# Each query-major score tile of self-attention made twice into its bank, in a decoder layer on one core

## The chip, the cores and the metric

The kernel runs on one core of one Trainium2 chip. The metric is the device time of one execution in microseconds; lower is better. "Before" is the kernel as it stands, "after" the kernel with the change below.

## What is computed

One decoder layer in fp32 for 4 sequences of 256 tokens and 128 channels: self-attention with l2-normed queries and keys, cross-attention with relative positions, and a top-1 mixture of 8 experts, each with a residual and a layer norm. The change lies in the self-attention:

```python
q = l2norm(q); k = l2norm(k)                         # over all 128 channels
q, k, v = (t.reshape(b, n, H, D).transpose(0, 2, 1, 3) for t in (q, k, v))   # H = 16 heads, D = 8
attn = jnp.einsum('bhnd,bhkd->bhnk', q * scale, k * scale) / temperature
attn = jax.nn.softmax(attn, axis=-1)
out = jnp.einsum('bhnk,bhkd->bhnd', attn, v)
```

## The kernel before

The five engines run programs of their own and meet at semaphores. What each does, and when, follows one table, ORDER, of steps "stage.step.batch": A1 and A2 are the self-attention of a batch, B its cross-attention and router, W work for later (blank stores, weight loads). Each engine goes through ORDER and takes the steps that concern it, in that order, so the work of up to three batches is interleaved on TensorE. After the table come the expert tiles (`up`, `down`).

The softmax needs each query's maximum over the keys. For that the scores are made query-major: step A1.d0 to A1.d15 of a batch, one tile per pair of heads and half of the queries. In `scores1` TensorE makes a tile with two matmuls (bf16 parts of the fp32 operands, 96 rows of contraction, 128 queries, 256 keys), one for each head, into the two halves of one bank of SA. VectorE reduces the bank to two negated maxima per query (`maxima`, L980). SA has two banks, and the tiles take them in turn together with the key-major tiles (A2.st0 to st15, `scores_t`, L1251, read by ScalarE's exponential at L761): `score_bank` makes TensorE wait until the tile two turns earlier has been read. The maxima are transposed (A1.shT, L1183), written to DRAM and read back as an extra row of the queries' operand, so that the key-major tiles come with the maximum already subtracted. Tiles of the exponential are multiplied with the values in `weigh1` (A2.pv, L1262).

Names that the rows show: SA the two score banks; negm the maxima; KS, QS the stacked operands of even batches and w_sb those of odd ones (they lie in the weights' room); MA and MB boxes of PSUM that one use after another fills; SB the four banks of cross-attention; L1345 and L1349 its scores, L1368 the subtraction of its maxima, L1051 its reduction, L1046 the maximum of two of its tiles, L801 and L798 its exponentials, L1380 its product with the values; L1215 the matmuls that stack the heads of batch 0, copied out by ScalarE (L708, L741); L1195 the projection of x; L603 the blank stores from P2b to sorted_x, issued by GpSimd when TensorE's count of score tiles has come to a point in ORDER; L425 SyncE's loads.

Of the kernel before, what the change touches and what calls it, by code (L numbers as in the profile page):

```python
# [13 lines left out]
NB, NT, C = 4, 256, 128  # L14
H, D = 16, 8
P = 128
# [6 lines left out]
SR = NTERM * D  # L23
# [32 lines left out]
def steps_of(text):  # L56
# [35 lines left out]
    B.tr5.3 W.v5.0 B.sc6.3 B.sh5.3 B.tr6.3 B.sc7.3 B.pv0.3 B.sh6.3 B.tr7.3 B.rk.2 B.sh7.3 B.nm0.3 B.pv1.3  # L92
    B.nm1.3 B.ln2.3 B.x2T.3 B.lg.3 B.rk.3
""")


A_FILLS = {"A1.qkv": ("qkv0", "qkv1"), "A1.qkT": ("qkT",), "A2.pv1": ("pv0",), "A2.nm0": ("norm0",), "A2.k2T": ("k2T",),
# [53 lines left out]
def column_a(g, j):  # L151

    return 8 * (j // 4) + 4 * g + j % 4
# [10 lines left out]
def build(nc, x_rows, x_cols, ctx_cols, wqkv_t, temperature, wproj_t, proj_b, wq_t, bq, wk_t, bk, wv_t, bv,  # L164
          er_t, router_w, router_b, w1, b1_cols, w2, b2, out):
    ctx = ExitStack()
    with ctx:
# [3 lines left out]
        def sb(name, shape, dt=FP32):  # L171
            return ctx.enter_context(nc.sbuf_tensor(name, shape, dt))

        def pb(name, shape, dt=FP32):
            return ctx.enter_context(nc.psum_tensor(name, shape, dt))

        def sem(name):
            return ctx.enter_context(nc.semaphore(name))
# [59 lines left out]
        QSs, KSs = (QS0, QS1), (KS0, KS1)  # L238
# [58 lines left out]
        start = sb("start", [P, E])  # L297
# [37 lines left out]
        def as_fp32(tile):  # L335
# [25 lines left out]
        SA = pb("SA", [P, 2, 512])  # L361
# [7 lines left out]
        s = {n: sem(n) for n in (  # L369

            "wqkv_in", "w_in", "temp_in", "c_in", "er_in", "fill", "stack0_fill", "pick_ok", "odd_ok", "ex_full", "ex_out", "v1_fill", "ident_ok", "consts", "er_split", "er_stacked", "bigw",
            "dchain", "pchain",

            "ma_full", "ma_free", "mb_full", "mb_free",

            "xT_in", "xtok_in", "n2_ok", "n2c_ok", "rn_ok", "qkn_ok", "v1_ok", "xpb_ok", "spa_ok", "pa_out", "qs_in",
            "stack_fill", "sa_full", "negm1_ok", "m_out0", "m_out1", "m_in0", "m_in1", "st_full", "exp1", "ve1_ok", "rs1_ok", "x1_ok",
# [801 lines left out]
        def _(pe):  # L1179
            mm = nc.tensor.matmul  # L1180
# [38 lines left out]
            def score_bank(name, b, u):  # L1219

                turn = TURN[name, b, u]
                if turn >= 2:
                    last_name, last_b, last_u = SCORES[turn - 2]
                    wait(pe, {"d": "negm1_ok", "st": "exp1"}[last_name], last_b * 16 + last_u + 1)
                return turn % 2

            def scores1(b, u):

                hp, qt = divmod(u, 2)
                if b == 0 and qt == 0:  # L1230
                    pe.wait_ge(s["ex_out"], hp + 1)
                if b > 0 and u == 0:
                    pe.wait_ge(s["qs_in"], b * 64)
                bank = score_bank("d", b, u)
                for i in range(2):
                    last = mm(SA[:, bank, i * NT:(i + 1) * NT], QSs[b % 2][0:2 * SR, column_a(i, hp), qt * P:(qt + 1) * P], KSs[b % 2][0:2 * SR, hp, :],  # L1236
                              start=True, stop=True)
                last.then_inc(s["sa_full"], 1)

            def transpose_shifts(b, a):  # L1240
# [4 lines left out]
            def scores_t(b, u):  # L1245

                hp, kt = divmod(u, 2)
                if u % 8 == 0:
                    pe.wait_ge(s[f"m_in{u // 8}"], b * 16 + 16)
                bank = score_bank("st", b, u)  # L1250
                mm(SA[:, bank, :], KSs[b % 2][:, hp, kt * P:(kt + 1) * P], QSs[b % 2][:, column_a(0, hp):column_a(1, hp) + 1:4, :], start=True, stop=True).then_inc(s["st_full"], 1)  # L1251

            def weigh1(b, grp):
                if grp == 0:
# [193 lines left out]
            def rank_then(b):  # L1448
                rank(b)
                keep_busy(b, "rk")  # L1450

            turns({
                ("A1", "qkv"): project_x, ("A1", "qkT"): transpose_q_k, ("A1", "ex"): stack_heads, ("A1", "d"): scores1, ("A1", "shT"): transpose_shifts,
                ("A1", "vcp"): first_weights, ("A2", "q2T"): project_q2,
                ("A2", "st"): scores_t, ("A2", "pv"): weigh1, ("A2", "nm"): transpose_o, ("A2", "oT"): o_to_cols,
                ("A2", "proj"): project_o, ("A2", "x1T"): x1_to_cols, ("A2", "k2T"): project_k2,
                ("B", "v"): project_v2, ("B", "gt"): stack_queries, ("B", "sc"): scores2, ("B", "tr"): transpose_scores, ("B", "sh"): shift,
# [92 lines left out]
```

## Time and profile before

| | |
|---|---|
| median of 3 runs | 312.88 us (311.1 to 313.0) |
| profiled execution | 311.56 us, span 309.8 us, 1.76 us around it |
| TensorE matmul busy | 247.2 us (80%), 3439 instructions |
| VectorE busy | 213.1 us (69%), 592 instructions |
| ScalarE busy | 137.1 us (44%) |
| mean granted TensorE clock | 0.888 |

A row of the timeline has the start in the span, the duration, the engine, line and operation, what is written from what, the shape, and how many instructions were merged into it; in brackets stands how long the engine was idle before it and what ended that. Matmuls overlap: of several in a row each shows its full latency, while their starts lie closer together.

### The profile page before, as it was taken

The page shows a single profiled execution, that of the slowest core. Times are in us where ns is not written, and L with a number is a line of the kernel's source. Part 1 is how long each engine was busy: PE and PEld are TensorE (multiplying, and loading weights), DVE is VectorE, ACT ScalarE, POOL GpSimd, SP SyncE. Part 2 cuts the span into 40 slices and gives each one's busy share as a digit, 9 for nine tenths or more (in the row PEclk, how much of TensorE's full clock was granted, in tenths as well). Part 3 has the DMA queues.
Part 4 walks back from the last instruction along what each step waited for, and adds up shares of the span by engine and source line. Part 5 has one row for each costly group of instructions (what it writes and reads, how often), then busy time and mean ns, then how long its engine had stood idle before and what let it go on. Part 6 is the DMA issues. An engine that isn't in the chain of part 4 may idle for free.

```text
span 309.8 us, 8568 instructions
## 1 busy us (share of the span) xinstructions
PE 247.2 (80%) x3439; PEld 185.4 (60%) x3440; DVE 213.1 (69%) x592; ACT 137.1 (44%) x318; POOL 81.0 (26%) x120
## 2 busy tenths in 40 slices
PE   3068797768999689997978999779786599999950
PEld 1037423322778466774867777569675359999950
DVE  8868955885677586797687745565343385899980
ACT  3127556306554445763332777523344213454420
POOL 8310400172011012074000030203103020456562
PEclk9999959955899989998779999995969958999995
DMA  2301488935688530269551013732710103499200
GB/s 68 118 0 51 160 288 215 254 91 95 168 226 220 146 51 20 87 190 234 90 133 26 4 49 92 138 104 45 263 38 9 29 17 87 132 307 359 83 6 1
DMA packets 28726, 36.36 MB, mean 117 GB/s; under 512 B 6039, under 2 KB 22405, under 8 KB 28016
## 3 DMA queue, kind: packets, MB, share of 16 engines
q1 hardware_dynamic: 24624, 23.67, 30.3%
q0 software_dynamic: 4064, 12.16, 11.7%
q8 instruction: 27, 0.44, 0.6%
q14 instruction: 11, 0.09, 0.1%
HBM read 24.41 MB, written 11.80 MB: 117 GB/s over the span
## 4 chain that ended last, share of the span: by engine, by line
PE 42%; DVE 9%; issue 5%; ACT 3%; DMA 3%; POOL 1%; SPq 1%; POOLq 0%; DVEq 0%; ACTq 0%
PE SB L1349 5%; PE SA L1488 5%; PE SB L1345 4%; PE SB L1488 4%; PE MB L1183 4%; PE SB L1496 3%; PE MB L1380 3%; PE SA L1323 2%; PE SB L1368 2%; DVE negm L980 2%; PE MA L1262 2%; DMA w_sb<-parts_a 2%; PE SA L1251 2%; PE SA L1236 2%; DMA parts_a<-SpA 1%
## 5 line engine op out<-in xcount | busy, mean ns | idle before, releaser
L980 DVE TENSOR_REDUCE negm<-SA 128x2 bf16<-128x512 f32 x64 | 41.4, 686 | 10.4 <-PE SA L1236 9.9
L761 ACT ACTIVATE P<-SA 128x512 f32<-128x512 f32 x64 | 35.8, 598 | 12.6 <-PE SA L1251 11.3
L708 ACT ACTIVATE Sb<-SB 128x512 bf16<-128x512 f32 x24 | 14.3, 597 | 36.0 <-PE SB L1349 35.9
L1051 DVE TENSOR_REDUCE negm<-MB 128x4 bf16<-128x512 bf16 x32 | 22.0, 687 | 9.2 <-PE MB L1183 8.9
L801 ACT ACTIVATE P2b<-SB 128x1024 f32<-128x1024 f32 x16 | 16.4, 1024 | 12.5 <-PE SB L1368 8.5
L654 POOL TENSOR_TENSOR rs<-ve,half 128x2 f32<-128x2 f32 x8 | 5.7, 712 | 57.2 <-DVE ve L941 57.2
L1046 DVE TENSOR_TENSOR Sm<-SB,Sb 128x512 bf16<-128x512 f32 x16 | 11.0, 688 | 13.9 <-ACT Sb L708 13.7
L1262 PE MATMUL MA<-P,V 128*32 128x256 f32 x256 | 19.0, 433 | 0.4 <-ACT qkT L708 0.4
L1368 PE MATMUL SB<-identb,negm 128*128 128x128 bf16 x192 | 18.0, 240 | 1.5 <-DVE negm L1051 1.5
L1236 PE MATMUL SA<-w_sb 96*128 96x256 bf16 x64 | 14.5, 332 | 5.7 <-DVE negm L980 3.6
L1195 PE MATMUL MA<-wqkv,xT 128*128 128x384 f32 x16 | 10.1, 726 | 10.0 <-ACT qkv L708 4.9
L695 POOL DMA_INDIRECT out<-P,token x15 | 15.4, 1030 | 6.0 <-issue 6.0
L1368 PEld LDWEIGHTS SB<-identb,negm 128*128 128x128 bf16 x192 | 13.9, 108 | 4.5 <-DVE negm L1051 2.9
L708 ACT ACTIVATE P<-MA 128x128 f32<-128x128 f32 x15 | 4.2, 278 | 28.0 <-PE MA L1183 19.0
L1349 PE MATMUL SB<-QZ,ErS 128*128 128x32 bf16 x384 | 15.8, 194 | 0.7 <-issue 0.7
L1349 PE MATMUL SB<-Z,ErS 128*128 128x32 bf16 x384 | 15.6, 194 | 0.0
L677 POOL DMA_INDIRECT sorted_x<-x,slot x8 | 8.2, 1024 | 27.9 <-DVE slot L1090 26.7
L1345 PE MATMUL SB<-QZ,KS 128*128 128x32 bf16 x384 | 13.8, 181 | 1.3 <-DVE QZ L1031 1.3
L690 POOL TENSOR_TENSOR rs<-ve,half 128x1 f32<-128x1 f32 x15 | 8.9, 595 | 20.6 <-DVE ve L1163 20.6
L1183 PE MATMUL MB<-identb,Sm 128*128 128x128 bf16 x96 | 10.0, 230 | 5.4 <-DVE Sm L1046 4.0
L1345 PEld LDWEIGHTS SB<-QZ,KS 128*128 128x128 bf16 x384 | 12.5, 100 | 2.4 <-issue 1.3
L1349 PEld LDWEIGHTS SB<-QZ,ErS 128*128 128x128 bf16 x384 | 13.4, 104 | 0.8 <-issue 0.8
(247 smaller groups left out, 607.9 us busy)
## 6 DMA issues: line engine op xcount, KB each, us to landing
sorted_x<-P2b POOLq DMA_DIRECT2D x4, 1161.0 KB, 6.7
w_sb<-in_w POOLq DMA_DIRECT2D x8, 512.0 KB, 4.7
w_sb<-in_w POOLq DMA_DIRECT2D x8, 256.0 KB, 4.3
w_sb<-parts_a SPq DMA_DIRECT2D x8, 192.0 KB, 4.0
parts_b<-SpB SPq DMA_DIRECT2D x8, 192.0 KB, 2.4
KZ<-parts_b SPq DMA_DIRECT2D x4, 384.0 KB, 5.3
Z<-parts_b SPq DMA_DIRECT2D x4, 384.0 KB, 5.5
KS<-parts_b SPq DMA_DIRECT2D x4, 384.0 KB, 5.5
```

What stands on the lines that cost most here:

```text
L708: return a.activation(dst, src, ACT.Copy)
L761: a.activation(P1[:, grp % 2, kt, 2 * i:2 * i + 2, :].rearrange("p h t -> p (h t)"), SA[:, bank_a("st", b, u), :], ACT.Exp).then_inc(s["ex ...
L801: a.activation(P2b[:, :, :, qs].rearrange("p k h q -> p (k h) q"), SB[:, at:at + 2, :].rearrange("p k (h q) -> p (k h) q", h=H), ACT.Exp). ...
L980: v.tensor_reduce(out=negm1[:, hp // 4, qt, :, hp % 4], in_=SA[:, bank_a("d", b, u), :].rearrange("p (g k) -> p g k", g=2), axis=AX.X, op= ...
L1051: v.tensor_reduce(out=negm2[:, qb, :], in_=MBb[:, 0:512].rearrange("p (c k) -> p c k", c=4), axis=AX.X, op=ALU.max, negate=True).then_inc( ...
L1183: return nc.tensor.transpose(dst, src, idn)
L1236: last = mm(SA[:, bank, i * NT:(i + 1) * NT], QSs[b % 2][0:2 * SR, column_a(i, hp), qt * P:(qt + 1) * P], KSs[b % 2][0:2 * SR, hp, :], sta ...
L1262: last = mm(MA[VW * i:VW * i + VW, (grp % 2) * NT:(grp % 2 + 1) * NT], V1[:, kt, h, :], P1[:, grp % 2, kt, i, :], start=(kt == 0), stop=(k ...
L1345: mm(bank[:, h, :], keys[:, h, kt * P:(kt + 1) * P], queries[:, h, QB * qb:QB * (qb + 1)], start=(h == 0), stop=False, skip_group_check=True)
L1349: last = mm(bank[:, :, q:q + 2], ErS[:, w:w + P], queries[:, :, QB * qb + q:QB * qb + q + 2], start=False, stop=False, skip_group_check=True)
L1368: last = mm(SB[:, banks_b(qb)[kt], c * P:(c + 1) * P], negm2[:, qb, c:c + 1].broadcast_to([P, P]), identb[:, :], start=False, stop=True, s ...
L1488: last = mm(UP[par][bank][:, k * P:(k + 1) * P], weights[:, at:at + P], xgT[:, par, :], start=True, stop=True)
```

## The change

Each of the 64 query-major tiles (16 in each of 4 batches) is made twice in a row by the same two matmuls into the same bank. Both rounds have start=True, so the second overwrites the first; the semaphore that releases VectorE is raised by the last matmul of the second round. The key-major function has the same loop, but no key-major step is in the table, so it runs once. Nothing is moved: each engine keeps its order. The lines of the changed file lie 15 or more further down.

```diff
+TWICE = frozenset("""
+    A1.d0.0 A1.d1.0 A1.d2.0 A1.d3.0 A1.d4.0 A1.d5.0 A1.d6.0 A1.d7.0 A1.d8.0 A1.d9.0 A1.d10.0 A1.d11.0 A1.d12.0
...
+def times(stage, step, b):
+
+    return 2 if f"{stage}.{step}.{b}" in TWICE else 1
...
                 bank = score_bank("d", b, u)
-                for i in range(2):
-                    last = mm(SA[:, bank, i * NT:(i + 1) * NT], QSs[b % 2][0:2 * SR, column_a(i, hp), qt * P:(qt + 1) * P], KSs[b % 2][0:2 * SR, hp, :],
-                              start=True, stop=True)
+                for _ in range(times("A1", f"d{u}", b)):
+                    for i in range(2):
+                        last = mm(SA[:, bank, i * NT:(i + 1) * NT], QSs[b % 2][0:2 * SR, column_a(i, hp), qt * P:(qt + 1) * P], KSs[b % 2][0:2 * SR, hp, :],
+                                  start=True, stop=True)
                 last.then_inc(s["sa_full"], 1)
```

## Rows read from the trace of the kernel before

**Rows 1.** The page: busy time, and the chain by engine.

```profile
PE 247.2 (80%) x3439; PEld 185.4 (60%) x3440; DVE 213.1 (69%) x592; ACT 137.1 (44%) x318; POOL 81.0 (26%) x120
...
PE 42%; DVE 9%; issue 5%; ACT 3%; DMA 3%; POOL 1%; SPq 1%; POOLq 0%; DVEq 0%; ACTq 0%
```

**Rows 2.** Line L1236: durations in ns (min/median/max), and what ended its waits.

```profile
L1236 PE MATMUL SA<-KS,QS x64: 269/273/418, 25.4 to 118.8; 96*128 96x256 bf16 x64
...
  DVE negm L980: 15.9, 30
```

**Rows 3.** Timeline, batch 0's tiles: VectorE.

```profile
33.14 3.81 DVE L980 TENSOR_REDUCE negm<-SA 128x2 bf16<-128x512 f32 x6 [0.37 <-PE SA L1236]
```

**Rows 4.** Timeline, batch 0's tiles: TensorE.

```profile
30.38 0.82 PE L1215 MATMUL SB<-SpA,P2b 128*96 128x256 bf16 x6
...
35.24 0.90 PE L1236 MATMUL SA<-KS,QS 96*128 96x256 bf16 x4 [0.37 <-DVE negm L980]
37.01 0.22 PE L1183 MATMUL MA<-identb,negm 128*16 128x128 bf16 x1 [0.86 <-DVE negm L980]
```

**Rows 5.** Timeline, batch 1's tiles: TensorE.

```profile
53.76 0.39 PE L1236 MATMUL SA<-w_sb 96*128 96x256 bf16 x2 [0.65 <-DVE negm L980]
...
67.14 1.20 PE L1236 MATMUL SA<-w_sb 96*128 96x256 bf16 x4 [1.90 <-DVE negm L980]
68.54 1.21 PE L1236 MATMUL SA<-w_sb 96*128 96x256 bf16 x4 [0.19 <-DVE negm L980]
```

**Rows 6.** Timeline, batch 1's tiles 8 to 15: VectorE.

```profile
66.40 5.47 DVE L980 TENSOR_REDUCE negm<-SA 128x2 bf16<-128x512 f32 x8
```

**Rows 7.** A window at batch 2's tiles 0 to 3: us, PE, PEld, DVE, ACT, POOL, clock, DMA.

```profile
90.20:94.50 4.30, 4.28 (x94) 3.78 (x91) 3.19 (x7) 1.89 (x4) 0.72 (x1) 1.00 0.45 116
```

**Rows 8.** Timeline, batch 2's tiles 3 to 9: TensorE, ScalarE, GpSimd.

```profile
94.10 0.38 PE L1236 MATMUL SA<-KS,QS 96*128 96x256 bf16 x2
...
94.78 0.75 POOL L603 DMA_DIRECT2D sorted_x<-P2b  x1 [2.89 <-PE SA L1236]
...
103.83 1.02 ACT L801 ACTIVATE P2b<-SB 128x1024 f32<-128x1024 f32 x1 [3.85 <-DMA sorted_x<-P2b]
...
105.78 0.91 PE L1195 MATMUL MA<-wqkv,xT 128*128 128x384 f32 x2 [3.02 <-ACT qkv L708]
...
109.16 1.06 PE L1236 MATMUL SA<-KS,QS 96*128 96x256 bf16 x4
```

**Rows 9.** Timeline, TensorE behind batch 2's tiles 11 and 12.

```profile
115.05 0.62 PE L1368 MATMUL SB<-identb,negm 128*128 128x128 bf16 x8 [0.20 <-DVE negm L1051]
```

**Rows 10.** Timeline, batch 3's tiles: TensorE.

```profile
144.83 1.03 PE L1236 MATMUL SA<-w_sb 96*128 96x256 bf16 x4 [1.70 <-DMA w_sb<-parts_a]
...
158.66 0.61 PE L1183 MATMUL MB<-identb,Sm 128*128 128x128 bf16 x4 [1.40 <-DVE Sm L1046]
...
162.85 0.39 PE L1236 MATMUL SA<-w_sb 96*128 96x256 bf16 x2 [0.31 <-DVE negm L980]
```

**Rows 11.** Windows at half clock: us, busy of PE, PEld, DVE, ACT, POOL, clock, DMA.

```profile
62.80:79.80 17.00, 13.35 (x55) 4.88 (x59) 12.25 (x27) 5.53 (x11) 8.02 (x15) 0.50 0.43 90
...
107.10:110.50 3.40, 3.40 (x65) 2.98 (x62) 1.49 (x4) 2.44 (x7) 1.02 (x1) 0.50 1.07 207
...
158.30:161.70 3.40, 3.04 (x25) 2.78 (x26) 2.88 (x5) 1.02 (x1) 0.00 (x0) 0.50 0.65 133
```

**Rows 12.** Timeline, TensorE: a key-major tile and a step weigh1 at either clock.

```profile
42.42 3.52 PE L1262 MATMUL MA<-P,V 128*32 128x256 f32 x32
...
75.28 0.61 PE L1251 MATMUL SA<-w_sb 128*128 128x512 bf16 x1 [0.16 <-ACT P L761]
...
86.47 0.39 PE L1251 MATMUL SA<-w_sb 128*128 128x512 bf16 x1 [0.16 <-ACT P L761]
...
77.58 3.01 PE L1262 MATMUL MA<-P,V 128*32 128x256 f32 x32 [0.41 <-ACT qkT L708]
...
88.13 1.93 PE L1262 MATMUL MA<-P,V 128*32 128x256 f32 x32
```

More of the change, by code:

```diff
@@ L94 @@
 """)
+TWICE = frozenset("""
+    A1.d0.0 A1.d1.0 A1.d2.0 A1.d3.0 A1.d4.0 A1.d5.0 A1.d6.0 A1.d7.0 A1.d8.0 A1.d9.0 A1.d10.0 A1.d11.0 A1.d12.0
+    A1.d13.0 A1.d14.0 A1.d15.0 A1.d0.1 A1.d1.1 A1.d2.1 A1.d3.1 A1.d4.1 A1.d5.1 A1.d6.1 A1.d7.1 A1.d8.1 A1.d9.1
+    A1.d10.1 A1.d11.1 A1.d12.1 A1.d13.1 A1.d14.1 A1.d15.1 A1.d0.2 A1.d1.2 A1.d2.2 A1.d3.2 A1.d4.2 A1.d5.2
+    A1.d6.2 A1.d7.2 A1.d8.2 A1.d9.2 A1.d10.2 A1.d11.2 A1.d12.2 A1.d13.2 A1.d14.2 A1.d15.2 A1.d0.3 A1.d1.3
+    A1.d2.3 A1.d3.3 A1.d4.3 A1.d5.3 A1.d6.3 A1.d7.3 A1.d8.3 A1.d9.3 A1.d10.3 A1.d11.3 A1.d12.3 A1.d13.3 A1.d14.3
+    A1.d15.3
+""".split())
+def times(stage, step, b):
+    return 2 if f"{stage}.{step}.{b}" in TWICE else 1
 A_FILLS = {"A1.qkv": ("qkv0", "qkv1"), "A1.qkT": ("qkT",), "A2.pv1": ("pv0",), "A2.nm0": ("norm0",), "A2.k2T": ("k2T",),
@@ L1250, in scores_t @@
                 bank = score_bank("st", b, u)
-                mm(SA[:, bank, :], KSs[b % 2][:, hp, kt * P:(kt + 1) * P], QSs[b % 2][:, column_a(0, hp):column_a(1, hp) + 1:4, :], start=True, stop=True).then_inc(s["st_full"], 1)
+                for _ in range(times("A2", f"st{u}", b)):
+                    last = mm(SA[:, bank, :], KSs[b % 2][:, hp, kt * P:(kt + 1) * P], QSs[b % 2][:, column_a(0, hp):column_a(1, hp) + 1:4, :], start=True, stop=True)
+                last.then_inc(s["st_full"], 1)
             def weigh1(b, grp):
```

## The prediction

> **What bounds the kernel now.** I read the page first, then the line of the doubled matmul, then the timeline around each batch's tiles, engine by engine. TensorE is busy for 80% of the span and holds 42% of the chain that ended last [rows 1]; VectorE reduces each tile. So the question for each of the 64 tiles is which of three things runs there: TensorE without a pause (then the added matmuls are paid in full), the loop over the two banks (then a part of them), or an engine or a transfer that TensorE waits for anyway (then nothing).
>
> **What one tile more costs.** A matmul of this line lasts 269 ns and more, at most 418 [rows 2], but matmuls overlap, and it is the distance of their starts that counts. A pair at full clock takes 0.38 us to its end [rows 8]; less 0.27 that is 0.11 from start to start. Four at half clock take 1.06 us [rows 8], so (1.06 - 0.42)/3 = 0.21. The change adds 2 matmuls to each tile: 0.21 us at full clock, 0.43 at half clock, and as much to the time until VectorE may begin. 64 times 0.21 is 13.7 us, which is the added issue time if the clock were full all along. The weight loads are the same weights again and run beside the matmuls. Nothing else is added, no wait and no transfer.
>
> **Batch 0 (25.4 to 37.0 us): bank loop.** VectorE makes 6 reductions in 3.81 us [rows 3]: (3.81 - 0.69)/5 = 0.62 a tile, 1.25 for a pair of tiles. That looks like VectorE's bound, but TensorE's rows show that it is just as much the loop of one bank: a reduction of 0.69, some 0.06 to 0.15 until TensorE starts, 0.38 for the tile, 0.04 until VectorE reads, together 1.2 to 1.26. VectorE therefore has no reserve of its own that would hide the second round; the loop grows by 0.21 to about 1.47. Where six matmuls of L1215 stand between two pairs of tiles (0.82 us to the end of the last, so 0.11 from start to start [rows 4]), TensorE alone needs 8 + 6 matmuls of 0.107 = 1.50 for what now takes 1.25. Seven such steps by 0.22, and 0.1 for the first pair: **+1.6 us**. TensorE waits 0.86 us for the last reductions before it can go on [rows 4], so the stretch is on the path. Bounds: 7 times 0.05 (were the six matmuls and the pauses to take it all) = 0.4, and 16 times 0.21 = 3.4.
>
> **Batch 1, tiles 0 to 7 (52.5 to 58.8).** TensorE waits for the banks again, 0.65 us before tile 2 [rows 5], and other steps of the same batch (the transposes of the outputs, the projection) stand between the tiles. Tile 0 comes 0.21 later, the loop of its bank adds 0.15 to 0.21 once more before each of two VectorE steps that the projection needs; the rest lies in the waits: **+0.6**, bounds 0.2 and 8 times 0.21 = 1.7.
>
> **Batch 1, tiles 8 to 15 (64.2 to 72), at half clock.** The first two are made long before VectorE is free: TensorE then waits 1.90 us [rows 5], so their second round is hidden. The other six are three rounds of the bank loop. It shows best here: TensorE starts at 67.14 and 68.54 [rows 5], 1.40 apart, which is 0.69 + 0.06 + 0.60 + 0.04, and VectorE's 8 reductions take 5.47 [rows 6]. At half clock the loop grows by 0.43 to 1.82. 3 times 0.43 and a remainder for the last tile: **+1.5** if the clock stays as it is. Bounds 0 and 8 times 0.43 = 3.4.
>
> **Batch 2, tiles 0 to 7 (90 to 101.5).** Up to 94.5 TensorE is busy 4.28 of 4.30 us [rows 7], so tiles 0 to 3 cost their full 4 times 0.21 = **+0.85**. Then comes a transfer: the last blank store is issued at 94.78, once tile 3 is made, ScalarE waits for it 3.85 us until 103.83, and TensorE behind it 3.02 us until 105.78 [rows 8]. Whatever tiles 4 to 7 add between 98.6 and 101.5, 0.85 us in all, disappears in those 3.02 us: **0**. Without that cover it would be 0.85.
>
> **Batch 2, tiles 8 to 15 (109 to 119).** Tiles 8 and 9 stand in an unbroken row of matmuls at half clock [rows 8]: 2 times 0.43 = **+0.85** (0.43 at full clock). Behind tiles 10 to 14 TensorE waits for VectorE's other reduction (0.20 us before 115.05 [rows 9], with the bank waits of tiles 12 to 14 before and behind it), and tile 15 lies beside a copy of ScalarE: **0**, at most 6 times 0.21 = 1.3.
>
> **Batch 3 (144.8 to 168).** Tile 0 begins when its operands land, after a wait of 1.70 us, and again at half clock: four matmuls take 1.03 [rows 10]. Tiles 0 to 2 add 1.28, of which some 0.2 lie in the wait for a bank: +1.1. Tile 3 is on the path, tile 4 keeps VectorE supplied and counts no further: +0.2. Tiles 5 to 7 end in TensorE's wait of 1.40 us for VectorE before 158.66 [rows 10]: 0. Tiles 8 and 9 are at half clock among matmuls of cross-attention: +0.85. Tiles 10 to 12 push the bank wait of 0.31 [rows 10] along: +0.3. Tiles 13 to 15: +0.45. Together **+2.9**, bounds 1.5 and 16 times 0.21 plus 5 times 0.21 for the tiles at half clock = 4.4. After 168 us there are no such tiles and everything moves as one.
>
> **The sum at the old clocks** is 1.6 + 0.6 + 1.5 + 0.85 + 0.85 + 2.9 = +8.3 us.
>
> **The clock.** From 62.8 to 79.8 us TensorE has half clock and is busy 13.35 of 17.0 us; the stretch 107.1 to 110.5, with 3.40 of 3.40, ends at once, and so does 158.3 to 161.7 with 3.04 of 3.40 [rows 11]. All three follow a stretch in which TensorE waited. With the second round, tiles 10 to 15 leave TensorE next to no pause (8 matmuls of 0.213 = 1.71 in a loop of 1.82), which the rows of the two short stretches liken to those that ended. So I take it that full clock comes back around tile 14 and not at 79.8. That returns 0.4 at tiles 14 and 15; 3.01 - 1.93 = 1.1 in the step that multiplies with the values [rows 12]; and some 0.5 in the key-major tiles, whose matmul is 0.61 - 0.39 = 0.22 shorter [rows 12], in two to three rounds of their loop. **-2.0.** The forecast is 8.3 - 2.0 = +6.3: 311.56 + 6.3 = **317.9 us** for an execution like the profiled one, which is 1.3 us below the median of the runs shown; 317.9 is 1.6% above that median. I give it without an addition for that, since one of those runs lies at 311.1.
>
> The Trainium skill says in "TensorE: Matmul & The Clock Gate", part 1, that "the default state is throttled, and activity releases the throttle". By that rule an added matmul can pay for itself. The trace agrees as far as its half-clock stretches follow waits; it cannot show how much more activity would have sufficed.
>
> **The rivals.**
> (a) The clock does not come back earlier: +8.3 at the old clocks, 319.9 us. For it: in the 17 us at half clock TensorE was already busy for 79% of the time [rows 11] and the clock stayed down.
> (b) Not slower: the clock. Besides the stretch above, TensorE's added work keeps the clock up at 107.1 to 110.5 and 158.3 to 161.7, where it is busy all the time [rows 11] and so would need about half: 1.7 + 1.5 us, of which 2 times 0.85 less 0.43 each, 0.85, was counted above as half-clock cost of the tiles and goes too; and 1.5 at batch 0's multiplication with the values, which took 3.52 us [rows 12]. 6.3 - 3.2 - 0.85 - 1.5 = +0.7, 312.3 us. It decides from where the added rounds fill the waits ahead of those stretches; the waits of 3.02 and 1.40 us [rows 8, 10] are longer than the 0.85 and 0.64 added in front of them, which speaks against it. In part it gives 314 to 316.
> (c) VectorE hides nearly all of it: the tiles wait for VectorE, not it for them. Then only the 4 + 2 + 4 tiles with TensorE unbroken count: about +2.5, 314 us. Against it: the loop of 1.40 us in batch 1 leaves VectorE idle between pairs of reductions.
> (d) All on the path: waits that I took for cover are loops that stretch along. 13.7 plus 0.21 for each of some 15 tiles at half clock: +17, 328 us. Against it: the 3.02 us behind the blank store.
> (e) The second round isn't made, or runs beside something: the program order of the changed kernel shows it as instructions of its own, 256 instead of 128. 312 us.
>
> **How the numbers follow.** Forecast 0.53 (315.9 to 319.5), (a) 0.18, (b) 0.14, (c) 0.08, (d) 0.06, (e) 0.01. The range from 313.0 to 322.5 holds the forecast, (a) with the bounds of the single stretches, (c) and the milder half of (b), and leaves out (d) and the rest. About 1%, 3.1 us, is what a measurement of this kernel can tell from no change. Slower by over 1% means above 316.0: most of the forecast, (a) and (d): 0.75. Within 1%: (b), (c), (e) and the lower edge of the forecast: 0.22. Faster: 0.03, if (b) goes further than worked out.
>
> **What the profile after would show.** TensorE's line with 256 matmuls, its starts 0.11 apart; batch 0's reductions no longer end to end but in pairs 1.47 apart; the blank store issued 3 to 4 us later than 94.78, with TensorE's wait behind it shorter by about 0.85; no longer wait behind tiles 5 to 7 of batch 3; and the half-clock stretch of batch 1 shorter than 17 us. Wrong would be: VectorE's last 6 reductions of batch 0 in the same 3.8 us, or a clock that falls and rises elsewhere by more than the sum.

## The result, and the profile after

| | before | after |
|---|---|---|
| median | 312.9 us, 4 runs (311.1 to 313.0) | 319.72 us, 4 runs (318.52 to 321.75) |
| profiled execution, span | 311.56 us, 309.8 us | 321.75 us, 320.0 us |
| mean granted TensorE clock | 0.888 | 0.913 |

The ratio is 1.027, with an interval of 1.020 to 1.034: slower. A repeat on one of the chips of the experiments, below, gave 1.012 (1.003 to 1.022). The medians differ by 6.8 us; the forecast was 6.3 us over the profiled execution, 317.9 us, and 319.72 lies inside the range of 313.0 to 322.5. Ratios below are made from undisturbed executions alone, so they are not always the quotient of the medians given with them. The unchanged kernel spreads more than those four runs show: on the three chips of the experiments its executions took 307.8 to 323.5 us.

The page after, its busy times and its chain by engine (before: [rows 1]):

```profile
PE 256.5 (80%) x3567; PEld 197.8 (62%) x3568; DVE 213.9 (67%) x592; ACT 136.8 (43%) x318; POOL 81.1 (25%) x120
...
PE 55%; DVE 16%; DMA 10%; issue 7%; ACT 5%; SPq 3%; POOL 1%; another core or an unknown queue 1%; POOLq 0%; ACTq 0%; DVEq 0%
```

TensorE has 128 matmuls more and 9.3 us more of busy time, and 12.4 us more of weight loads, which run beside the matmuls; the other engines are within 0.8 us of before. The line of the doubled matmul, durations in ns and then its waits and who waited for it:

```profile
L1252 PE MATMUL SA<-KS,QS x128: 269/272/289, 25.4 to 126.8; 96*128 96x256 bf16 x128
...
  DVE negm L995: 8.1, 18
...
  DVE negm L995: 18.0, 22
```

The first of the two waits is TensorE's for VectorE's reductions, the second VectorE's for TensorE. The first has halved, from 15.9 us in 30 places [rows 2] to 8.1 in 18, and the second has grown from 9.9 us to 18.0. The 15.9 and 8.1 count the weight load and the matmul behind it both; of the matmuls alone the wait fell from 4.8 to 2.1 us. A part of the second round lies in that difference. The rest is paid. Batch 0, VectorE and then TensorE (before: [rows 3, 4]):

```profile
34.68 1.29 DVE L995 TENSOR_REDUCE negm<-SA 128x2 bf16<-128x512 f32 x2 [0.55 <-PE SA L1252]
36.21 1.29 DVE L995 TENSOR_REDUCE negm<-SA 128x2 bf16<-128x512 f32 x2 [0.24 <-PE SA L1252]
37.68 1.29 DVE L995 TENSOR_REDUCE negm<-SA 128x2 bf16<-128x512 f32 x2 [0.18 <-PE SA L1252]
```

```profile
34.04 1.04 PE L1252 MATMUL SA<-KS,QS 96*128 96x256 bf16 x8
34.91 0.82 PE L1230 MATMUL SB<-SpA,P2b 128*96 128x256 bf16 x6
35.57 1.07 PE L1252 MATMUL SA<-KS,QS 96*128 96x256 bf16 x8
37.05 1.12 PE L1252 MATMUL SA<-KS,QS 96*128 96x256 bf16 x8 [0.41 <-DVE negm L995]
39.03 0.27 PE L1198 MATMUL MA<-identb,negm 128*16 128x128 bf16 x1 [0.86 <-DVE negm L995]
41.85 1.03 PE L1268 MATMUL SA<-QS,KS 128*128 128x512 bf16 x2 [2.55 <-DMA QS<-shift_a]
```

Six reductions that ran end to end in 3.81 us now come in pairs 1.53 and 1.47 us apart, with VectorE waiting for TensorE in between. On TensorE 8 + 6 matmuls fill 34.04 to 35.57, the 1.53 of the pairs, and the wait of 0.86 us ahead of the transposition is the same as before: the stretch moved as one. The last row is a wait that the forecast did not have, 2.55 us for the read of the maxima; it is followed up below.

Batch 1, VectorE and TensorE at half clock (before: [rows 5, 6]):

```profile
72.94 0.69 DVE L995 TENSOR_REDUCE negm<-SA 128x2 bf16<-128x512 f32 x1 [0.54 <-PE SA L1252]
...
74.76 0.69 DVE L995 TENSOR_REDUCE negm<-SA 128x2 bf16<-128x512 f32 x1 [0.27 <-PE SA L1252]
...
76.58 0.69 DVE L995 TENSOR_REDUCE negm<-SA 128x2 bf16<-128x512 f32 x1 [0.27 <-PE SA L1252]
```

```profile
68.84 1.91 PE L1252 MATMUL SA<-w_sb 96*128 96x256 bf16 x8
71.86 5.54 PE L1252 MATMUL SA<-w_sb 96*128 96x256 bf16 x24 [1.11 <-DVE negm L995]
...
83.83 1.93 PE L1280 MATMUL MA<-P,V 128*32 128x256 f32 x32 [0.41 <-ACT qkT L723]
...
98.62 0.61 PE L1252 MATMUL SA<-KS,QS 96*128 96x256 bf16 x4 [3.06 <-DMA KS<-parts_a]
```

Every second reduction stands 1.82 us behind the one before, against 1.40 of the bank's loop before, and 24 matmuls make a row without a pause. The wait behind tiles 8 and 9 fell from 1.90 to 1.11 us: their second round was hidden. At 83.83 full clock was back, and the step that multiplies with the values took 1.93 us, against 3.01 before [rows 12]; in the four other profiles with this batch doubled the step stood wholly in half clock and took 3.64. The last row is another wait that before did not have, ahead of tile 0 of batch 2.

Batches 2 and 3, GpSimd, ScalarE and TensorE (before: [rows 8, 10]):

```profile
103.98 0.75 POOL L618 DMA_DIRECT2D sorted_x<-P2b  x1 [4.28 <-PE SA L1252]
```

```profile
110.61 1.02 ACT L816 ACTIVATE P2b<-SB 128x1024 f32<-128x1024 f32 x1 [0.51 <-PE SB L1386]
```

```profile
113.91 0.91 PE L1210 MATMUL MA<-wqkv,xT 128*128 128x384 f32 x2 [0.66 <-ACT qkv L723]
...
152.89 1.05 PE L1252 MATMUL SA<-w_sb 96*128 96x256 bf16 x8 [1.04 <-DMA w_sb<-parts_a]
...
165.52 0.61 PE L1198 MATMUL MB<-identb,Sm 128*128 128x128 bf16 x4 [1.18 <-DVE Sm L1061]
165.92 1.06 PE L1252 MATMUL SA<-w_sb 96*128 96x256 bf16 x4
```

The blank store was issued 9.2 us later than before, at 103.98, and had landed when ScalarE needed it at 110.61: ScalarE waited for TensorE instead (0.51, against 3.85 for the store before), and TensorE's wait behind it fell from 3.02 to 0.66. The wait for VectorE ahead of tiles 8 and 9 of batch 3 fell only from 1.40 to 1.18, less than the 0.64 that the prediction put into it. The windows at half clock and one of the stretches that were at half clock before (us, busy of PE, PEld, DVE, ACT, POOL, clock, DMA; before: [rows 11]):

```profile
66.40:83.40 17.00, 14.64 (x49) 6.53 (x49) 11.01 (x25) 5.08 (x11) 8.06 (x15) 0.50 0.42 90
165.40:168.80 3.40, 3.28 (x24) 2.79 (x25) 2.12 (x5) 0.92 (x1) 0.00 (x0) 0.50 0.86 159
112.00:120.00 8.00, 7.25 (x158) 5.90 (x157) 6.14 (x14) 3.88 (x12) 1.02 (x1) 1.00 0.54 124
```

TensorE was busy for 14.64 of 17.00 us instead of 13.35, and half clock still lasted 17.00 us. The page and these rows already decide three of the signs named beforehand: VectorE's pairs 1.47 us apart came, a half-clock stretch shorter than 17 us did not, and the blank store was later by 9.2 instead of 3 to 4 us, 3.1 of it from the wait ahead of batch 2.

### The profile page after: what moved, and what is told of

Its sections match the earlier page's. It is cut to its first block, busy times and chain, and to the rows that moved or that the text cites. A ratio compares the mean times of both kernels' runs of the same rounds, so it can differ in the third digit from the quotient of the medians.

```text
span 320.0 us, 8824 instructions
## 1 busy us (share of the span) xinstructions
PE 256.5 (80%) x3567; PEld 197.8 (62%) x3568; DVE 213.9 (67%) x592; ACT 136.8 (43%) x318; POOL 81.1 (25%) x120
## 3 DMA queue, kind: packets, MB, share of 16 engines
q0 software_dynamic: 4064, 12.16, 11.2%
## 4 chain that ended last, share of the span: by engine, by line
PE 55%; DVE 16%; DMA 10%; issue 7%; ACT 5%; SPq 3%; POOL 1%; another core or an unknown queue 1%; POOLq 0%; ACTq 0%; DVEq 0%
PE SA L1252 7%; PE SB L1367 6%; PE SA L1506 5%; PE SB L1363 5%; PE MB L1198 4%; PE SB L1506 4%; PE MB L1398 4%; DMA w_sb<-parts_a 4%; PE SB L1514 3%; DVE negm L995 3%; PE SA L1268 3%; SPq L440 3%; PE MA L1198 2%; DMA KS<-parts_a 2%; PE MA L1210 2%
## 5 line engine op out<-in xcount | busy, mean ns | idle before, releaser
L995 DVE TENSOR_REDUCE negm<-SA 128x2 bf16<-128x512 f32 x64 | 42.4, 688 | 18.5 <-PE SA L1252 18.0
L723 ACT ACTIVATE Sb<-SB 128x512 bf16<-128x512 f32 x24 | 14.3, 597 | 41.1 <-PE SB L1367 38.5
L1252 PE MATMUL SA<-w_sb 96*128 96x256 bf16 x128 | 22.2, 319 | 3.9 <-DMA w_sb<-parts_a 2.0
L1061 DVE TENSOR_TENSOR Sm<-SB,Sb 128x512 bf16<-128x512 f32 x16 | 11.0, 688 | 16.6 <-ACT Sb L723 15.5
L1252 PE MATMUL SA<-KS,QS 96*128 96x256 bf16 x128 | 17.7, 273 | 3.9 <-DMA KS<-parts_a 3.1
L1252 PEld LDWEIGHTS SA<-w_sb 96*128 96x128 bf16 x128 | 12.6, 111 | 11.1 <-DVE negm L995 5.3
L1386 PE MATMUL SB<-identb,negm 128*128 128x128 bf16 x192 | 16.7, 228 | 1.3 <-DVE negm L1066 1.3
L710 POOL DMA_INDIRECT out<-P,token x15 | 15.5, 1031 | 6.0 <-issue 6.0
L1280 PE MATMUL MA<-P,V 128*32 128x256 f32 x256 | 16.3, 383 | 0.4 <-ACT qkT L723 0.4
L1252 PEld LDWEIGHTS SA<-KS,QS 96*128 96x128 bf16 x128 | 11.2, 97 | 7.6 <-DMA KS<-parts_a 3.2
L1386 PEld LDWEIGHTS SB<-identb,negm 128*128 128x128 bf16 x192 | 13.0, 103 | 4.4 <-DVE negm L1066 2.9
L1268 PE MATMUL SA<-QS,KS 128*128 128x512 bf16 x32 | 12.3, 428 | 3.7 <-DMA QS<-shift_a 2.5
```

The source lines that it names most:

```text
L723: return a.activation(dst, src, ACT.Copy)
L995: v.tensor_reduce(out=negm1[:, hp // 4, qt, :, hp % 4], in_=SA[:, bank_a("d", b, u), :].rearrange("p (g k) -> p g k", g=2), axis=AX.X, op= ...
L1268: last = mm(SA[:, bank, :], KSs[b % 2][:, hp, kt * P:(kt + 1) * P], QSs[b % 2][:, column_a(0, hp):column_a(1, hp) + 1:4, :], start=True, s ...
L1386: last = mm(SB[:, banks_b(qb)[kt], c * P:(c + 1) * P], negm2[:, qb, c:c + 1].broadcast_to([P, P]), identb[:, :], start=False, stop=True, s ...
```

## The experiments

They were asked four things: which batches carry the cost, whether the places called covered are covered, whether the new waits for transfers belong to the change, and what more rounds do. Lengths of stages are the time between the first matmuls of two steps, named by their starts in the trace of before. "Unchanged" and "doubled" tell whether the tiles of that very stage were made twice; so each kernel says something on each stage.

**One batch at a time.** In `times`, and the same with 1, 2 and 3:

```diff
-    return 2 if f"{stage}.{step}.{b}" in TWICE else 1
+    return 2 if b == 0 and f"{stage}.{step}.{b}" in TWICE else 1
```

> Only the 16 tiles of batch 0 are made twice. If the stages add as in the sum: +1.6 to +2.0 us. If the second cause seen in the trace of the full change holds (the read of the first half of the maxima lands late behind the blank store, and later operand reads with it), +3 to +4. If every added matmul is paid at its issue time: +3.4.

> Only batch 1. Sum by stages: +2.1 at the old clocks, near +0.1 if the clock returns earlier behind tiles 8 to 15. Every added matmul paid: +3.4 at full clock, +5.1 with half of them at half clock.

> Only batch 2. Sum by stages: +1.3 to +1.7, of which 0.85 ahead of the blank store's gate and 0.4 to 0.85 at tiles 8 and 9. Every added matmul paid: +3.4. In the profile TensorE's wait behind the blank store should be about 0.85 shorter than the 3.02 us of before.

> Only batch 3. Sum by stages at the old clocks: +2.9. If the added rounds lift TensorE's clock there, as the profile of the full change shows for this batch: about 0. Every added matmul paid: +3.4.

On one chip, where the kernel before had a median of 314.16 us:

| doubled | median us | ratio (interval) |
|---|---|---|
| batch 0 | 316.74 | 1.010 (1.003 to 1.017) |
| batch 1 | 317.45 | 1.012 (0.998 to 1.027) |
| batch 2 | 314.71 | 1.004 (0.997 to 1.011) |
| batch 3 | 316.12 | 1.002 (0.996 to 1.009) |

The four add up to 2.9%, which agrees with 2.7% for all together. Only batch 0 is told from nothing by its own interval; the order of the four is not settled by the times, so the stages had to say it.

**Covered and uncovered tiles.** The 16 tiles that the prediction put at nothing, and then the other 48:

```diff
-    return 2 if f"{stage}.{step}.{b}" in TWICE else 1
+    return 2 if int(step[1:] if step[1:].isdigit() else -1) in {1: (8, 9), 2: (4, 5, 6, 7, 10, 11, 12, 13, 14, 15), 3: (4, 5, 6, 7)}.get(b, ()) and f"{stage}.{step}.{b}" in TWICE else 1
```

> Only the 16 tiles are made twice that the prediction put at nothing (batch 1: 8 and 9; batch 2: 4 to 7 and 10 to 15; batch 3: 4 to 7). Cover theory: 0, within 0.7 us. Every added matmul paid: 16 times 0.21 = +3.4 us.

> Only the other 48 tiles are made twice. Cover theory: the whole cost of the change, +6 to +8.5 us. Every added matmul paid: three quarters of it, +5 to +6.4.

The 16 gave 312.21 us against 313.82, ratio 0.999 (0.993 to 1.005); the 48 gave 317.09, ratio 1.016 (1.010 to 1.022), which is +5.0 us. Had all 16 been paid (3.4 us, 1.011), the first interval would not hold it. The whole time alone doesn't settle it, though, since the clock differed as well: in the executions behind the two ratios (5 to 10 of each kernel) the mean granted clock was 0.920 with the 16 tiles doubled, 0.907 without doubling and 0.909 with the 48. A straight line through the 77 executions of the unchanged kernel gives some 2 us less for 0.01 more of mean clock (an estimate), so a cost of 2 us could hide there. The stages settle it where the clock is equal: in the profile with the 16 doubled, batch 1 from 64.2 to 71.4 took 7.23 us, against 7.24 before, and batch 3 from 152.0 to 158.7 took 6.77, against 6.62 to 6.75 unchanged. The choice of covered tiles was right; that all others are uncovered was not, as the stages below show.

**Four rounds.**

```diff
-    return 2 if f"{stage}.{step}.{b}" in TWICE else 1
+    return 4 if f"{stage}.{step}.{b}" in TWICE else 1
```

> All 64 tiles made four times, three added rounds of 0.21 us. By stages (bank loop, TensorE unbroken, cover): batch 0 +6, batch 1 +2.5 and +1.5 to +6 by the clock, batch 2 +2, batch 3 +7, together +19 to +24 us. Every added matmul paid: +41. If the clock pays the added work back: under +15, with a mean clock well above that of the changed kernel.

338.7 us, ratio 1.083 (1.075 to 1.090), +25.9 us, above the 19 to 24 expected. That is more than three times the cost of one added round (17 to 20) and less than three times 13.7. The mean granted clock was 0.938 in the executions behind the ratio, against 0.907 without doubling. In batch 0 VectorE waits before every reduction; timeline of VectorE, and a window with the columns as above:

```profile
33.82 0.69 DVE L995 TENSOR_REDUCE negm<-SA 128x2 bf16<-128x512 f32 x1 [0.84 <-PE SA L1252]
34.70 0.69 DVE L995 TENSOR_REDUCE negm<-SA 128x2 bf16<-128x512 f32 x1 [0.18 <-PE SA L1252]
36.23 0.69 DVE L995 TENSOR_REDUCE negm<-SA 128x2 bf16<-128x512 f32 x1 [0.84 <-PE SA L1252]
```

```profile
26.00:44.00 18.00, 17.99 (x161) 15.63 (x159) 10.41 (x15) 6.37 (x20) 3.19 (x4) 1.00 0.14 57
```

TensorE is busy for 17.99 of 18.00 us, and the stage from 25.8 to 37.0 takes 17.73 us: +6.5 for three added rounds, where one cost 1.6. The stage holds 14 of the tiles, 14 times 0.214 = 3.0 us a round: of one round 1.4 us were covered, of three (9.0) 2.5. So the cover is a fixed amount that the first round uses up in part; once it is gone, TensorE's own time is the price. With which round it ends no run shows, since none has three.

**The new wait for the maxima.** In the kernel after, the read of the first half of the maxima into QS is issued at 35.88, behind the first blank store (W.bl0.0, at 35.39), and TensorE waited 2.55 us for it. In the kernel before it stands behind that store too (33.81 and 33.63), without such a wait. With batch 0 doubled and the store in this place four profiles show the wait, 1.51 to 2.55 us, and a fifth (loads later) does not. With only batch 0 doubled that store was moved behind two more tiles in ORDER; then the same move was made in the kernel before, without any doubling:

```diff
-A1.d10.0 A1.d11.0 W.bl0.0 A1.ex7.0 A1.d12.0 A1.d13.0 W.v6.0
+A1.d10.0 A1.d11.0 A1.ex7.0 A1.d12.0 A1.d13.0 W.bl0.0 W.v6.0
```

> Batch 0 alone made twice, and the first blank store issued behind tile 13 instead of tile 11, so behind the read of the first maxima and not ahead of it. If the late landing of that read costs time: TensorE's wait of 2 us before the first key-major tile is gone and the time is 1 to 2 us below that of batch 0 alone. If the wait is made good before tile 0 of batch 1 anyway: the wait is gone and the time is the same as with batch 0 alone, +1.6 to +3.

> No tile is made twice; only the first blank store is issued behind tile 13 instead of tile 11. If its place matters only together with the later tiles of the changed kernel: the same as before, within 0.5 us. If it costs time in either kernel: 1 to 2 us faster than before, and then the 0.8 us between batch 0 alone and its version with the later store says nothing of the doubling.

With batch 0 doubled: 315.68 against 313.82, ratio 1.002 (0.995 to 1.009). Without doubling: 315.9 against 313.73, ratio 1.006 (1.000 to 1.012). The wait is gone; timeline of TensorE in the first of the two:

```profile
39.30 0.22 PE L1198 MATMUL MA<-identb,negm 128*16 128x128 bf16 x1 [0.86 <-DVE negm L995]
39.45 0.91 PE L1268 MATMUL SA<-QS,KS 128*128 128x512 bf16 x2
```

But the way from 37.0 to 52.5 took 16.5 us with the store moved and 16.5 us with it in its old place. Over all profiles that way takes 15.5 to 17.8 us where batch 0 is unchanged and 14.8 to 17.6 where it is doubled: the wait for the maxima only takes the place of the wait that ends the stretch anyway, the one for the operands of batch 1. That one shows in the profile with only batch 3 doubled, where the first 55 us are the unchanged kernel's; timeline of TensorE:

```profile
54.84 1.03 PE L1252 MATMUL SA<-w_sb 96*128 96x256 bf16 x4 [4.08 <-DMA w_sb<-parts_a]
```

The same wait was 0.20 us in the profile of before, which is the exception: three more profiles that run the same instructions up to there had 3.37 to 4.35. So the wait of 2.55 us is caused by the change, or by the load at that moment, but it costs nothing that can be seen. The later store by itself does no good, and the second run says that it may cost some 0.5%. So the 315.68 is no sign that the wait was worth anything.

**The new wait ahead of batch 2.** In the kernel after, two weight loads were issued just when the operands of batch 2 were read; timeline of GpSimd, and of SyncE with the first and the last of the four reads:

```profile
89.73 0.59 POOL L635 DMA_DIRECT2D w_sb<-in_w  x1 [13.39 <-PE SA L1268]
90.32 0.57 POOL L641 DMA_DIRECT2D w_sb<-in_w  x1
```

```profile
89.85 0.34 SPq L440 DMA_DIRECT2D QS<-parts_a  x1
...
91.17 0.43 SPq L440 DMA_DIRECT2D KS<-parts_a  x1
```

The loads were moved away from the operands' reads, in the kernel before and in the kernel after, and the kernel after was run again unaltered on the same chip:

```diff
-A2.st14.0 W.u0.0 A2.st15.0 A2.pv2.0 A2.pv3.0 A1.d0.1 A1.d1.1 A1.d2.1
+A2.st14.0 A2.st15.0 A2.pv2.0 A2.pv3.0 A1.d0.1 A1.d1.1 W.u0.0 A1.d2.1
...
-A2.st12.1 W.u1.0 W.v7.0 B.sc2.0
+A2.st12.1 B.sc2.0
...
-A1.d8.2 A1.d9.2 B.tr6.0
+A1.d8.2 A1.d9.2 W.u1.0 W.v7.0 B.tr6.0
```

> No tile is made twice; three weight loads (W.u0 behind tile 1 of batch 1, W.u1 and W.v7 behind tile 9 of batch 2) are issued after the operand reads of batches 1 and 2 have landed, not beside them. If the reads that share the DMA engines with those loads set the start of tile 0: 1 to 3 us faster than before, and the last read of batch 1 lands some 4 us after its issue, not 6. If TensorE is late anyway: the same.

> The full change with the same later loads. If the wait of 3.06 us before tile 0 of batch 2 in the profile after comes from the loads: the wait is under 0.5 us, and the time is 2 to 3 us below that of the full change, +4 to +6 against before. If it comes from the doubled tiles themselves: the wait stays.

> The full change once more on the same chip as the three others. Stages by theory (bank loops, TensorE unbroken, cover) without a gain from the clock: +6 to +8 us. With displaced reads on top: +9 to +11. The profiles tell whether the wait before tile 0 of batch 2 and the one before the first key-major tile are there each time.

On this chip the kernel before had a median of 313.73 us.

| kernel | median us | ratio (interval) |
|---|---|---|
| before, loads later | 312.43 | 0.994 (0.989 to 1.000) |
| after, loads later | 317.59 | 1.016 (1.009 to 1.024) |
| after, again | 318.93 | 1.012 (1.003 to 1.022) |

With the loads later, tile 0 of batch 2 starts without a wait (timeline of TensorE):

```profile
95.72 0.60 PE L1252 MATMUL SA<-KS,QS 96*128 96x256 bf16 x4
```

Without the move it does so too, in the second profile of the kernel after; timeline of TensorE, then of SyncE (the last read) and of GpSimd (the first load):

```profile
98.04 0.60 PE L1252 MATMUL SA<-KS,QS 96*128 96x256 bf16 x4
```

```profile
91.96 0.43 SPq L440 DMA_DIRECT2D KS<-parts_a  x1
```

```profile
92.37 0.59 POOL L635 DMA_DIRECT2D w_sb<-in_w  x1 [14.90 <-PE SA L1268]
```

So the 3.06 us do not belong to the doubled tiles as such: the stage from 80.5 to 90.2 took 12.93 us there, and 9.73 in the repeat, as in the kernel before (9.71). What the profiles with the wait have in common is the order of the transfers. In the repeat both loads were issued behind the last read. Over the 14 profiles a wait of over 1 us stands ahead of this tile in just the three where both loads were issued before the last of the four reads: the kernel after (3.06), batch 0 alone (1.56, stage 11.44) and four rounds (3.04). That speaks for the loads, as was expected of them. But the kernel after came out with either order, and whether the change makes the bad one more frequent, so few profiles don't say. In both profiles with the loads later the stretch from 106.5 to 119.5 took 14.0 us (at full clock) and 14.3 (6.8 us of it at half clock), against 12.6 at its shortest, so the move seems to give something back elsewhere. In the kernel after it has no gain that these runs can tell. With them the kernel before has the lowest ratio of all that were tried, by 0.6%, and its interval ends just below 1.

## Why the prediction was right

Stages, in us. The doubled ones are from the kernel after, its repeat, its version with the loads later, and the experiments that doubled that batch. Where the clock differs between profiles, equal clocks are compared.

| stage | predicted | unchanged | doubled | measured |
|---|---|---|---|---|
| batch 0, 25.8 to 37.0 | +1.6 | 11.2 to 11.7 | 12.8 | +1.6 |
| batch 1, tiles 0 to 7, 52.5 to 58.3 | +0.6 | 5.76 | 6.37 | +0.6 |
| batch 1, tiles 8 to 15, 64.2 to 80.5, half clock | +1.5 | 7.24 + 9.74 | 8.52 + 9.97 | +1.5 |
| batch 2, tiles 0 to 7, 90.2 to 106.5 | +0.85 | 16.2 (mean of 7) | 16.0 (mean of 4) | 0 |
| batch 2, tiles 8 to 15, 106.5 to 119.5, full clock | +0.85 | 12.6 to 12.7 (see below) | 12.6 | 0 |
| batch 3, tiles 0 to 2, 144.8 to 147.8, full clock | +1.1 | 1.86 to 1.90 | 2.29 to 2.41 | +0.4 |
| batch 3, tiles 3 to 7, 152.0 to 158.7 | +0.2 | 6.62 to 6.75 | 6.99 | +0.3 |
| batch 3, tiles 8 to 12, 158.7 to 163.2, half clock | +1.15 | 4.24 to 4.51 | 5.44 to 5.58 | +1.0 |
| batch 3, tiles 13 to 15, 165.1 to 167.9 | +0.45 | 2.82 | 3.25 | +0.4 |
| sum | +8.3 | | | +5.8 |

5.8 us by stages, 6.8 us between the first medians (ratio 1.027), 5.2 us between those of the repeat (ratio 1.012, which is 3.9 us), 6.3 us forecast: the range and the size held, and the reason, TensorE's own time less what waits cover, is what the stages show. Most terms came out within 0.2 us. But that the total is so near is luck: two steps of the forecast failed in opposite directions by about as much.

**What held.** The start-to-start time of 0.21 us for two matmuls at full clock and 0.43 at half. Batch 0 as the loop of a bank, with steps of 1.53 us behind six matmuls (predicted 1.50). The 1.82 us of the loop in batch 1: both its stages together grew by 1.5 in the four profiles with it doubled and at half clock throughout, against unchanged ones at the same clock. Tiles 8 and 9 of batch 1 and the 16 covered tiles together: nothing (0.999). Tiles 8 to 15 of batch 3: +1.4 at half clock (+1.05 at full, where the stage from 158.7 went from 3.31 to 3.94), predicted 1.6.

**The first step that failed: batch 2.** The prediction put tiles 0 to 3 at their full 0.85, since TensorE was busy "4.28 of 4.30 us", and tiles 4 to 7 at nothing. TensorE does get later by it: the stage from 90.2 to 95.2 grew from 5.0 to 5.6 in every profile with it doubled. It was given back before 106.5. What ends that stretch is not TensorE but the blank store, and the store is not of one length: from its issue to ScalarE's release it took 9.05 us in the profile of before, 7.97 to 9.45 in six others without doubling in this batch, and with all 16 tiles doubled 7.46 and 8.61, and twice 6.6 or less, where ScalarE no longer waited for it (once in the kernel after, once in its version with the loads later). So 0.85 was laid over a transfer that varies by more. Whether the store is faster because it is issued later, beside other traffic, or by chance, is not settled by four profiles against seven; nor can they exclude a few tenths of cost there. The measured entry is 0 with an uncertainty of some 0.4 us. The profile in which tiles 0 to 3 were doubled and tiles 4 to 7 not had 15.0 us, the shortest of all. With four rounds ScalarE waited for TensorE there and no longer for the store, and the stage took 19.5 us: that much more was not given back.

Tiles 8 and 9 were priced at half clock in an "unbroken row of matmuls". At full clock the row isn't unbroken. It shows in the profile of the 16 covered tiles, where tiles 8 and 9 are made once; timeline of TensorE:

```profile
112.03 0.60 PE L1252 MATMUL SA<-KS,QS 96*128 96x256 bf16 x4
113.16 0.40 PE L1198 MATMUL MB<-identb,Sm 128*128 128x128 bf16 x4 [0.53 <-DVE Sm L1061]
```

and in the kernel after, where they are made twice:

```profile
111.29 1.04 PE L1252 MATMUL SA<-KS,QS 96*128 96x256 bf16 x8
112.16 0.39 PE L1198 MATMUL MB<-identb,Sm 128*128 128x128 bf16 x4
```

TensorE waited 0.53 us for VectorE right behind the two tiles, and the second round took that wait's place: 12.58 us for the stretch in both, and in the profile of the 48, where tiles 8 and 9 are made twice and 10 to 15 once. No profile with all eight made once was at full clock throughout; the nearest, with batch 1 doubled, took 12.66 with its first 1.8 us at half clock. Only at half clock, where TensorE comes later, does it cost: 13.56 in the repeat of the kernel after, against 12.9 to 13.0 in three profiles without doubling there whose half clock fell on the same tiles. The same goes for tiles 0 to 2 of batch 3, priced at +1.1 by a profile that was at half clock there; most others had full clock, and there it is +0.4. In all the sum was 2.5 us too large.

**The second step that failed: the clock, -2.0.** The prediction took it that with the pauses gone full clock would come back around tile 14 of batch 1. It did not. Windows of the repeat of the kernel after and of the kernel with batch 1 doubled (columns as above), in this order:

```profile
67.90:88.30 20.40, 17.99 (x81) 7.85 (x80) 14.18 (x28) 5.71 (x11) 8.09 (x15) 0.50 0.39 87
```

```profile
67.30:87.70 20.40, 18.23 (x89) 8.20 (x90) 14.06 (x27) 5.96 (x13) 8.03 (x15) 0.50 0.42 98
```

At 88 and 89% busy, with 24 matmuls in one row, half clock lasted 20.4 us, longer than the 17.0 of before. The other profiles agree: it lasted 20.4 us in four of the five with tiles 10 to 15 of batch 1 doubled, and in the eight profiles with those tiles made once it lasted 17.0 us in seven and 13.7 in one. Only in the first profile of the kernel after was it back a little earlier with respect to the work: the stage from 71.4 to 80.5 took 8.27 us there and 9.97 to 9.98 in the four other profiles with batch 1 doubled. On the mean of all, that stage took 9.35 us with the tiles made once and 9.63 with them doubled, so the clock gave back nothing there. The 3.01 us from which the forecast took its 1.1 was a mixture as well: half clock ended within that step, which took 3.64 us where it stood wholly in half clock. Rival (a), which kept the old clocks, was right on this step, by the reason given for it. The sentence of the Trainium skill that I brought ("TensorE: Matmul & The Clock Gate", part 1: activity releases the throttle) is not borne out at this place by one added round; with three added rounds, in one profile, the stage was at full clock throughout and took 7.09 us. Over the whole run the sentence of the Trainium skill fits two kernels, four rounds (0.938) and the 16 covered tiles (0.920), both against 0.907 without doubling on the same chip, and not the change itself: 0.911 in the repeat and 0.909 with the loads later, against 0.910 without doubling, all in the executions behind the ratios (3 to 10 of each kernel). Why the clock was higher with the 16 covered tiles and not with all 64 stays open. In single profiles the mean granted clock was 0.888 to 0.916 in four profiles of kernels with at most the 16 covered tiles doubled, and 0.896 to 0.913 in four with 48 or 64.

**The rivals.** (b) and (c) fall with the first ratio and with the stages; the repeat's interval alone, 1.003 to 1.022, would have left (c) and a part of (b). (d), all on the path, falls with the covered tiles. (e), no second round, falls with 256 matmuls on the line. (a) as a whole gave 319.9, nearer to the first median of 319.72 than the forecast; it shares the sum of 8.3, which the stages don't bear out, and the repeat has 318.93 beside a kernel before that had 313.73. Which of the two numbers is nearer the truth is within what the runs can tell.

**Why the first profile showed +10.2 us.** Of the 10.2 us between the two profiled spans some 5.8 are the change. The wait ahead of batch 2 was 3.2; the way from 37.0 to 52.5 took 17.3 us against 15.5, and the stage from 167.9 to 203.9, which has none of these tiles, 37.4 against 36.0, where the profile of before was the shortest of all (37.3 to 38.0 in every other one). Against that, 2.0 came back where before had been at half clock (144.8 to 152.0 was 1.6 shorter, though the change adds 0.4 there), and 1.1 where after left half clock earlier (71.4 to 80.5 was 0.8 shorter, though the change adds 0.2). The rest is in pieces of 0.5 us and less. The profile of before was a good draw in two stretches, that of after a bad one in one.

## What to carry to other kernels

Price added work by who is waited for at its place, tile by tile: the loop of a buffer and unbroken rows pay in full, a wait behind the work takes it for nothing, and the cover is a fixed amount, so a second helping costs more than the first. Before a single profile's waits for transfers and its half-clock stretches go into a sum, ask whether they would stand in the next execution; a term that rests on one of them has its variation as its error. A new wait in the trace is no cost until the stage around it has grown, and grown in more than one profile. And look at the mean clock of the executions beside their times: a kernel with added work can have the better clock, and then "the same time" is not "no cost".

## What the runs showed of the hardware

- A TensorE busy for 18.23 of 20.40 us kept half clock all that time. Such a stretch lasted 20.4 us in four of the five profiles with tiles 10 to 15 of batch 1 made twice, and 17.0 us or less in the eight with them made once.
- The same blank store of 1161 KB took from 6.6 us or less to 9.45 us from its issue until its reader went on, in 13 profiles of kernels that all make it behind tile 3 of batch 2.
- The wait for batch 1's operands was 0.20 us in one profile and 3.37 to 4.35 in four others of the same instructions up to there, and 1.16 and 2.26 with a store or with loads moved; what the reads meet on their way was not separated. The unchanged kernel's executions spread over 5%, 307.8 to 323.5 us.
- TensorE waited 3.06, 1.56 and 3.04 us for batch 2's operands in the three profiles where two weight loads were issued before the last of its four reads, and not at all, or 0.04 us, in the eleven others.
